# Pieces of the projections between first and second scores, and the quantised weights' steps some half groups sooner, in a two-layer gated cross-attention kernel

## The reference

```
x = x + tanh(g_xattn[0]) * pruned_attention(norm(x), ctx)      # keeps the 460 keys of 512 with the largest column sums
x = x + tanh(g_ffn[0])   * fp4_mlp(norm(x))                    # 256 -> 704 -> 256, blocks of 16 rounded to fp4
x = x + tanh(g_xattn[1]) * linear_attention(ctx, norm(x))      # k^T v per head, no softmax, then a norm
x = x + tanh(g_ffn[1])   * int8_linear(norm(x))

pruned_attention: scores = softmax(q k^T / 4)                  # [8, 16, 512, 512]
                  col_sum = sum(scores, over queries); mask = top_k(col_sum, 460)
                  out = (scores * mask) v, then Wo
fp4_mlp:          wq = fp4(w) for w_gate, w_up, w_down too: scale = max|block| / 6, round to a grid of 8 values
```

## Time and profile before

| | |
|---|---|
| median of 3 runs | 1168.69 us (1166.48 to 1169.58) |
| the profiled execution | 1172.58 us |
| its span | 1170.9 us |
| busy in the span | PE 90%, DVE 85%, ACT 77%, POOL 29% |
| steps 42 to 227 in it | from 128 to 598 us |
| first scores of step 236, of step 255 | 617.02 us, 669.14 us |
| mean granted clock of TensorE | 0.962 |

### The profile page before, as it was taken

One profiled execution on the slowest core, in us unless ns is written; L12 is line 12 of the kernel. 1 busy time (PEld: TensorE's weight loads), 2 busy tenths in 40 slices (PEclk: granted clock), 3 DMA queues, 4 the chain that ended last, 5 costly groups with the idle time before them and its releaser, 6 DMA issues.

```text
span 1170.9 us, 17921 instructions
## 1 busy us (share of the span) xinstructions
PE 1052.1 (90%) x5580; PEld 474.5 (41%) x5580; DVE 993.5 (85%) x1903; ACT 897.6 (77%) x2032; POOL 345.0 (29%) x512
## 2 busy tenths in 40 slices
PE   7888999999999999999987777899999999999964
PEld 5332322322222322322321122346676777677642
DVE  7688888998898988988998947468999999999955
ACT  4577798999999999999999844765676677667644
POOL 7524123122122131131112886002222222222112
PEclk9897999999999999999998887999999999999986
DMA  8623421332233123303204101010121112110001
GB/s 278 144 68 78 127 61 33 101 97 75 59 101 96 44 71 100 93 19 100 69 26 110 56 16 40 10 46 27 28 63 37 46 36 59 42 46 19 28 9 37
DMA packets 76267, 75.99 MB, mean 65 GB/s; under 512 B 11860, under 2 KB 67980, under 8 KB 76172
## 3 DMA queue, kind: packets, MB, share of 16 engines
q1 hardware_dynamic: 76172, 74.84, 23.2%
HBM read 47.02 MB, written 27.28 MB: 63 GB/s over the span
## 4 chain that ended last, share of the span: by engine, by line
PE 55%; ACT 20%; DVE 15%; issue 6%; POOL 2%; DMA 1%; SPq 0%; DVEq 0%; ACTq 0%; POOLq 0%
PE ps_a L1733 13%; ACT ea L1440 9%; PE ps_b L1689 8%; PE ps_s L1292 8%; ACT prob L1454 6%; DVE nmax L1352 6%; PE ps_s L1312 3%; PE ps_s L1689 3%; PE ps_a L1254 3%; PE ps_b L1254 2%; PE ps_f L1704 2%; PE ps_a L1742 2%; PE ps_f L798 2%; PE ps_f L1767 2%; PE ps_f L769 1%
## 5 line engine op out<-in xcount | busy, mean ns | idle before, releaser
L1440 ACT ACTIVATE ea<-ps_a,nmax 128x512 f32<-128x512 f32 x512 | 354.0, 714 | 59.2 <-DVE nmax L1352 58.6
L1352 DVE TENSOR_REDUCE nmax<-ps_a 128x2 f32<-128x1024 f32 x256 | 311.6, 1219 | 53.5 <-PE ps_a L1254 51.4
L1292 PE MATMUL ps_s<-ea,rz 128*32 128x512 f32 x1024 | 259.9, 624 | 13.4 <-DVE rank L1381 11.4
L1312 PE MATMUL ps_s<-prob,v_pad 128*32 128x512 f32 x1024 | 256.2, 626 | 6.1 <-DVE att L1406 3.4
L1454 ACT ACTIVATE prob<-ps_b 128x1024 f32<-128x1024 f32 x214 | 226.8, 1060 | 4.5 <-PE ps_b L1254 4.0
L1733 PE MATMUL ps_a<-wgu,xT 128*128 128x352 f32 x512 | 166.3, 465 | 3.3 <-ACT xT L1898 2.1
L1254 PE MATMUL ps_b<-q_st,k_st 52*128 52x512 f16 x512 | 106.7, 393 | 34.2 <-ACT prob L1454 22.6
L1440 ACT ACTIVATION_READ_ACCUMULATOR ea<-ps_a,nmax 128x1 f32 x512 | 119.0, 232 | 0.0
L1254 PE MATMUL ps_a<-k_st,q_st 48*128 48x512 f16 x512 | 101.5, 393 | 14.6 <-ACT ea L1440 11.6
L1733 PEld LDWEIGHTS ps_a<-wgu,xT 128*128 128x128 f32 x512 | 92.9, 191 | 52.5 <-issue 10.3
L1910 ACT ACTIVATE ea<-ps_a 128x352 f32<-128x352 f32 x128 | 59.5, 466 | 59.1 <-PE ps_a L1733 58.9
(11 more groups left out here) (259 smaller groups left out, 1810.6 us busy)
## 6 DMA issues: line engine op xcount, KB each, us to landing
k_scr<-k_p SPq DMA_DIRECT2D x24, 256.0 KB, 3.4
q_scr<-q_p SPq DMA_DIRECT2D x24, 256.0 KB, 2.8
q_st<-q_scr SPq DMA_DIRECT2D x32, 192.0 KB, 5.0
k_st<-k_scr SPq DMA_DIRECT2D x32, 192.0 KB, 5.4
cT<-in_ctx_T SPq DMA_DIRECT2D x8, 512.0 KB, 5.2
x_in<-in_x SPq DMA_DIRECT2D x8, 512.0 KB, 6.3
c_in<-in_ctx SPq DMA_DIRECT2D x8, 512.0 KB, 4.5
v_scr<-v_s SPq DMA_DIRECT2D x8, 512.0 KB, 4.9
```

What stands on the lines that cost most here:

```text
L1292: e.matmul(ps_s[q:q + 32, :], rz[:, t, r, 2 * k + h, o:o + 32], ea[g % RING][:, 2 * k + h], start=(n == 0 and (apart or k == 0)), stop=(n ...
L1312: e.matmul(ps_s[o:o + 32, :], v_pad[u % 2][:, t, 4 * r + 2 * k + h], at.prob[g % PROBS][:, 2 * k + h], start=(t == 0 and (apart or k == 0) ...
L1352: e.tensor_reduce(nmax[u % 2][:, t].rearrange("p (h r) -> p r h", h=2)[:, r], ps_a[:, z % 2 * 2:z % 2 * 2 + 2], AX_X, ALU.max, negate=True ...
L1440: e.activation(ea[c % RING][:, g % 4], ps_a[:, g % 4], ACT.Exp, bias=nmax[u % 2][:, t, n:n + 1], accum_out=tot[u % 2][:, t, n:n + 1]).then ...
```

## The change

In a step, the piece of a projection now stands between first and second scores instead of behind the values. The tables of the fp4 weights are moved: the loads by 5 steps, the first maxima by 5, the quarters by 5 growing to 11, the turns by 5 growing to 11 (two of them by 2, one by 1 the other way), and VectorE copies a turn out one step after TensorE made it instead of in the same step. `LOADS` (the next stage's first loads) and `OPENING` stay where they were.

```
-LARGEST_AT = 241, 245, 249
-QUARTER_AT = 243, 245, 247, 249, 251, 253, 255, 257, 259, 264, 267, 270, 273
-TURN_AT = 253, 254, 255, 256, 261, 262, 263, 264, 277, 280, 283
+LARGEST_AT = 236, 238, 246
+QUARTER_AT = 238, 240, 242, 244, 246, 248, 250, 252, 254, 256, 258, 260, 262
+TURN_AT = 248, 250, 252, 254, 259, 261, 263, 265, 268, 270, 272
...
-        def step(z):
+        def step(z, between):
             if z < ALL_Z:
                 first(z)
+            between()
             if z <= ALL_Z:
                 b = within(z - LAG - 1, ALL_Z)
                 if b is not None:
...
-    AHEAD, CLEAR, LOADS, OPENING = pj.ahead, 235, 244, 261
+    AHEAD, CLEAR, LOADS, OPENING = pj.ahead, 230, 244, 261
...
-                step(z)
-                for s, part in pj.at_turn.get(z, ()):
-                    fill(s, part)
+                def pieces():
+                    for s, part in pj.at_turn.get(z, ()):
+                        fill(s, part)
+
+                step(z, pieces)
...
-                if z in TURN_AT:
-                    n = TURN_AT.index(z)
+                if z - 1 in TURN_AT:
+                    n = TURN_AT.index(z - 1)
                     fp4.copy(e, n, fp4_bank(n))
```

## The result

The changed kernel takes 1190.34 us in the median of 4 runs (1185.45 to 1195.64) against 1169.13 us for the kernel before in the same comparison: a ratio of 1.0173, 95% interval 1.0140 to 1.0207. It is slower by some 20 us. The forecast was 1170.7 us and no difference, with 1158 to 1184 as its range; the time lies outside. The profiled execution of the changed kernel took 1185.45 us, with a span of 1183.6.

The account below looks back on a forecast made before the run. No engine bounds alone; the loop of first scores, maxima and exponential does, with 26.5 us left to TensorE in 470. 1172.6 + 3 - 1.5 + 0.5 = 1174.6, less 3.9 is 1170.7 us; range 1158 to 1184.

Parts of the forecast that it names:

- part one: Steps 42 to 227, pieces moved ahead of second scores: filled and made waits sum to +3 us, kept within -12 to +16.
- the low clock: TensorE's slower clock behind a stall: some us, named only for the weights' load stall; no term in steps 42 to 227.
- VectorE's places: Steps where a piece waits until VectorE empties the bank: +6 us for 5 places, +8 for 28 others.
- It fills waits: Steps 42 to 227: pieces fill TensorE's waits ahead of second scores (10 us) and column sums and values (7), -17 us.
- ScalarE's wait for maxima, down by more than half: Sign in the score loop that would show the forecast wrong and the kernel faster; the wait was 28.0 us.
- The nine places: Steps where a piece waits until ScalarE empties the bank: +13 us for TensorE, some 1.4 us each.
- what VectorE gives back: Steps 42 to 227: VectorE gets pieces and first scores sooner, so some maxima come earlier, -7 us.
- Steps before 42: No second scores there; a piece fills the column sums' wait for a rank copy in one step, -1.5 us.
- the bank's waits aren't covered: Slower rival, steps 42 to 227: second scores wait behind TensorE's wait for the bank, part one +18, 1184 us; chance 0.36.
- the faster rival: Steps 42 to 227: pieces fill more than they hold up, VectorE's places cost nothing, -11, about 1159 us; chance 0.27.
- The 30 gaps: Gaps over 0.1 us between first and second scores, all said to stand in steps without a piece, where TensorE runs ahead.
- Part two: The weights' steps: moved loads, first maxima and splits, with VectorE's stall 6.7 us and `rs_a` 3.8 late; +0.5, -3 to +6.

Follow-up runs that it names:

- e8_not_next_step: Kernel before, with pieces between first and second scores except in 45 steps from step 42 on where the projection before ended one step earlier; ratio 0.9941.
- e3_not_at_nine: Changed kernel, but in the nine steps whose bank ScalarE empties the piece stands behind the values as before; ratio 1.0000.
- e6_filled_wait: Changed kernel, with the second scores made three extra times ahead of the piece in the nine steps whose bank ScalarE empties; ratio 1.0098.
- e1_piece_alone: Changed kernel with the weights' tables, CLEAR and the copy of a turn as before, so only the pieces are moved; ratio 1.0159.
- the nine alone: Kernel before, with the piece between first and second scores only in the nine steps whose bank ScalarE empties; ratio 1.0083.
- part two alone: Changed kernel with the pieces behind the values as before, so only the tables, CLEAR and the copies are changed; ratio 1.0041.

## Why the prediction was wrong

**The sum of part one failed**: +3 for steps 42 to 227, measured +20.3. The loops of five kernels, one behind the other, put its terms on record:

| | loop, us | difference | forecast |
|---|---|---|---|
| before | 470.7 | | |
| 85 pieces whose bank is free a step earlier (`e8_not_next_step`) | 462.6 | -8.1 | -17 |
| and 36 where VectorE empties it (`e3_not_at_nine`) | 472.3 | +9.7 | +6, +8 and -7 |
| and 9 where ScalarE does, clock kept (`e6_filled_wait`) | 482.0 | +9.7 | +13 |
| and the low clock (`e1_piece_alone`) | 490.6 | +8.6 | 0 |

The third difference holds the added matmuls too, so the low clock is at least the fourth. The forecast of -17 was for all the pieces; the 85 fill 14.3 us, and what the 45 others fill besides is inside their two rows. The -7 was half of what VectorE's places cost, so it stands with them.

Two steps failed, each by some 9 us of the 17:

- **"It fills waits", -17**: mis-sized. The waits did go, 22.7 us to 2.6 in the changed kernel. But I took every filled microsecond as time, and the loop gave 8.1 for 14.3 filled: a part came back as TensorE's own waits ahead of pieces. With it I had misread a sign. ScalarE's wait for maxima, down by more than half, was to mean "faster"; it fell from 28.0 us to 2.6, and came back as a wait for second scores (2.7 us before, 12.3 in `e8_not_next_step`, 48.0 in the end). I had written that the gaps of TensorE and ScalarE bound the gain. As I read it now, the engines feed each other in a ring, and these gaps are one slack that can be spent once; the traces fit this, but no run tests it by itself.
- **The low clock, 0 in the sum**: left out without a reason. I had it only for the weights' stall, though the earlier trace rows showed 0.50 behind a stall. It was 8.6 us. With it alone the forecast would have been 1179, slower.

The other terms came nearer:

- **The nine places, +13**: right in mechanism and nearly in size, 10.4 alone. Too small was the wait, "some 1.4 us": it was 1.06 to 1.52 with the nine alone, but 1.74 to 2.02 beside the other moves. I had read it from a row of the order before, where the piece of the step before still stood behind the values. The bigger wait is also what the low clock followed.
- **VectorE's places, +14, and what VectorE gives back, -7**: together +7, measured 9.7, in 36 places where I had counted 33. The two weren't measured apart.
- **Steps before 42, -1.5**: -5.5 in the one trace, nothing that the times show.
- **The rival "the bank's waits aren't covered"**, with 0.36 the likeliest case, named the side and the mechanism. Its nearness in size is luck. Its terms add up to 1186, not to the 1184 that stands there, and need 0.6 us in each of 28 places: some 23 us for all of VectorE's places, where 9.7 were measured. The clock's 8.6 us, which it lacked, made up for most of that. The price of the faster rival is off by 2 us as well: -11 and +0.5 on 1168.7 are 1158.
- **The 30 gaps** ahead of second scores all stand in steps that have a piece, 26 of them behind a step without one. My sentence can be read the other way round; the sum needs it this way.
- **Part two, +0.5 (-3 to +6)**: +4.8 alone (1.8 to 6.4 per mille of the time: 2.1 to 7.5 us); beside part one 1.0173 against 1.0159, which can't be told from nothing. So it is inside its range. Foreseen were VectorE's stall (6.7; 5.6 and 7.5 measured) and `rs_a` 3.8 late (2.5, alone 4.4). The 3.3 given back behind `rs_a` are not shown: the trace of the changed kernel has 4.6 us less there, that of part two alone 2 us more, and these traces differ in the granted clock behind `rs_a`, 0.97 and 0.95 (before: 0.95). Missed was the other side of SP's exchange. I counted what the weights win when the keys and queries stand behind them, and not what these lose: 3.35 us for TensorE as soon as VectorE's own stall doesn't cover it.

## What to carry to other kernels

When a piece of work is moved into a gap, ask first whether it can find its own resource ready there: moving the 85 pieces that could made this kernel 0.6% faster, and moving 45 more that had to wait for a bank turned that into 1.6% slower. Before waits of several engines that feed each other in a ring are added up, ask whether they are one slack: here 14.3 us filled were worth 8.1. A wait that a change makes has to be read in the order after the change, with its neighbours moved, and what TensorE's clock does behind it belongs in the sum. Where something overtakes in a queue, price both: what comes sooner, and what is overtaken.

## What the hardware showed that was not expected

Waits of TensorE of 1.74 to 2.02 us in an otherwise busy stretch were followed by a low granted clock in 6 of 9 places (a pair of matmuls of 1.07 us for 0.62). Those of 1.06 to 1.52 us with the nine alone were not, and those of 1.52 to 1.64 us in 2 of 9. The length alone doesn't decide: behind step 99 the window's clock was 0.80 in the changed kernel and 1.00 in `e1_piece_alone`, with waits of 1.99 and 2.00 us, and behind step 102 it was 1.00 and 0.78, both times after 1.80 us. Six extra matmuls in each of the nine waits, whose results nobody uses, made the changed kernel some 0.7% faster (1.0098 against 1.0173 of the kernel before).
